# Stage one of an attention and mixture-of-experts layer: the input is also read in turned layout, and normalized there

## The chip, the core and the metric

The kernel runs on one core of one Trainium2 chip. TensorE (PE in the profile) multiplies matrices, VectorE (DVE) and ScalarE (ACT) work element by element, GpSimd (POOL) issues indirect DMAs and does some element work, and SyncE (SP) issues most DMAs. The metric is the device time of one execution in microseconds; lower is better.

## The reference, cut to what matters

```python
x = L0_attn_x                                    # (4, 2048, 512) f32
xn = _layernorm(x, axis=-1)                      # (x - mean) / sqrt(var + eps), over the 512 features
x = x + attention(xn, Wq, Wk, Wv, Wo) + moe(xn, gate_w, w_gate_up, w_down, ws_gate_up, ws_down)

# attention: q = xn @ Wq (16 heads of 32), k, v = xn @ Wk, xn @ Wv (4 heads), causal softmax, @ Wo
# moe:       logits = xn @ gate_w.T  -> best 3 of 8 groups -> softmax -> top 6 of 32 experts, 96 places each
#            + shared expert: silu(xn @ gs) * (xn @ us) @ ws_down
```

## The kernel before, in words

The 8192 tokens go through four stages: stage one (`stage_a`, to about 1100 us), the experts (`stage_m`, in part woven into what follows), attention (`stage_b`) and the output projection (`stage_c`). The change touches stage one alone.

Stage one goes over 16 chunks of 512 tokens. Chunk 0 and the last two are written out or run with their own flags; the others are one hardware loop. Every engine has its own program, and only semaphores order them. For a chunk TensorE multiplies the turned, normalized input (features on partitions, tokens along the row) with weights that stay in SBUF. All products are done in three terms of rounded f32: each operand is split into a high part (ACT copies it with rounding) and a low part (DVE subtracts the high part from the value), and the terms are high x high, high x low, low x high. In the order of TensorE's program, a chunk is:

- the gate logits (8 matmuls, `gate`), then V, four blocks of Q, and K (12 matmuls each, `product`), with two small groups of transposes (`smp`) in between;
- 11 products for the gate and up halves of the shared expert;
- the shared expert's down product: four groups of 17 matmuls into `yp`, one group for each 128 tokens, alternating between two PSUM banks. A group waits (`ysb_done`) until DVE has added the group two before it into `y_sb`.

The turned input of the next chunk is made during this last part. DVE has computed mean and variance of the next chunk's rows (`ln_stats`, `ln_variance`), the inverse deviation `rstd` (`ln_inverse`) and the normalized rows `xn` (`ln_scale`, line 577), 128 tokens on partitions by 512 features. `xn` is also written to DRAM for the experts. TensorE turns `xn` with 16 transposes of 128 x 128 (`transposes`, line 765) into the two PSUM banks `xtp`: eight ahead of the down product, eight between its second and third group. ACT rounds each 128 x 512 block of `xtp` into `x_hi` (line 449) once the chunk's last product has read the old `x_hi`; DVE subtracts it into `x_lo` (line 583). The next chunk's first matmul waits for all four blocks of `x_lo`.

SP's order in a chunk: load the rows of x to which the result is added (`y_sb`); store `qk_hi`, `qk_lo` (Q and K, five blocks of 128 x 512 each) and V; wait for `ln_done`; store `xn`; load the rows of the chunk after next; wait for DVE's additions; store the sum. POOL writes the expert table with 24 indirect DMAs a chunk.

Of the kernel before, what the change touches and what calls it, by code (L numbers as in the profile page):

```python
# [19 lines left out]
ALU = mybir.AluOpType  # L20
# [131 lines left out]
def stage_a(nc, t, car):  # L152

    ctx = ExitStack()
    with ctx:
# [107 lines left out]
        glu_done = sem("glu_done")  # L263
        hhi_done = sem("hhi_done")
        hlo_done = sem("hlo_done")
        xhi_done = sem("xhi_done")
        xlo_done = sem("xlo_done")
        ysb_done = sem("ysb_done")
# [35 lines left out]
        def earlier(n):  # L304

            return [m for m in range(n) if place[m] == place[n]]

        iota_e = cst[:, 0:E]
        tri = cst[:, E:E + NG * NG].rearrange("p (a b) -> p a b", b=NG)
        tok0 = cst[:, E + NG * NG:]  # L310
# [18 lines left out]
        def _(sp):  # L329
# [13 lines left out]
            def body(c, nxt, nxt2):  # L343
                sp.wait_ge(ysb_done, c * NT + 2)
                sp.sem_inc(sp_pass, 1)
                sp.dma_start(y_sb[:], chunk(x_d, c)).then_inc(xr_in, 16)
                if not nxt:
                    sp.wait_ge(xn_out, 16 * NC)
                    sp.wait_ge(xt_done, NC * KC)
                    load_weights(sp, t, 0, car["wgu0"], car["wdn0"], car["w_in"][0])  # L350
                sp.wait_ge(qlo_done, c * (NKV + 1) + NKV + 1)
                sp.sem_inc(sp_pass, 1)
                sp.wait_ge(qhi_done, c * (NKV + 1) + NKV + 1)
                sp.sem_inc(sp_pass, 1)
                sp.dma_start(columns(t["q_hi"], c), qk_hi[:, 0:NKV, :].bitcast(F32)).then_inc(qkv_out, 16)
                sp.dma_start(columns(t["q_lo"], c), qk_lo[:, 0:NKV, :].bitcast(F32)).then_inc(qkv_out, 16)
                sp.dma_start(columns(t["k_hi"], c), qk_hi[:, NKV:NKV + 1, :].bitcast(F32)).then_inc(qkv_out, 16)
                sp.dma_start(columns(t["k_lo"], c), qk_lo[:, NKV:NKV + 1, :].bitcast(F32)).then_inc(qkv_out, 16)
                sp.wait_ge(vt_done, c + 1)
                sp.sem_inc(sp_pass, 1)  # L360
                sp.dma_start(chunk(v_d, c), v_t[:]).then_inc(qkv_out, 16)
                if nxt:
                    sp.wait_ge(ln_done, c * NT + 2 * NT)
                    sp.sem_inc(sp_pass, 1)
                    sp.dma_start(chunk(xn_d, c + 1), xn[:]).then_inc(xn_out, 16)
                if nxt2:
                    sp.dma_start(x_sb[:], chunk(x_d, c + 2)).then_inc(x_in, 16)
                if not nxt:
                    sp.wait_ge(acc_done, NC * NACC)
                    for part in range(JC // 2):  # L370
                        load_qk(sp, t, car, 0, 0, part)
                if nxt:
                    sp.wait_ge(ysb_done, c * NT + NT + 2)
# [47 lines left out]
        def _(act):  # L421
# [20 lines left out]
            nc.scalar.activation(gw[:, :, 0:E], g_f[:], ACT.Copy).then_inc(g_hi_done, 1)  # L442
            whi(range(KC))

            def xhi(c, ks=range(KC)):

                for k in ks:
                    act.wait_ge(xt_done, c * KC + k + 1)
                    nc.scalar.activation(x_hi[:, k, :], xtp[:, k % 2, :], ACT.Copy).then_inc(xhi_done, 1)

            def logits(c):

# [43 lines left out]
                    xhi(c + 1)  # L496

            act.wait_ge(init_v, 1)
            xhi(0, (0, 1))
            whi(range(KC, NEAR))  # L500
            xhi(0, (2, 3))
            whi(range(NEAR, NEAR + 2))
            logits(0)
            whi(range(NEAR + 2, LATE))
# [11 lines left out]
        def _(dve):  # L516
# [54 lines left out]
            def ln_scale(c):  # L571
                dve.wait_ge(rstd_done, c * 5 + 5)
                dve.wait_ge(tab_init, 32)
                dve.wait_ge(xn_out, c * 16)
                dve.wait_ge(xt_done, c * KC)
# [4 lines left out]
            def xlo(c, ks=range(KC)):  # L580
                for k in ks:
                    dve.wait_ge(xhi_done, c * KC + k + 1)
                    V.tensor_tensor(x_lo[:, k, :], xtp[:, k % 2, :], x_hi[:, k, :].bitcast(F32),
                                    ALU.subtract).then_inc(xlo_done, 1)


# [13 lines left out]
            xlo(0, (0, 1))  # L600
            wlo(range(KC))
            xlo(0, (2, 3))
            wlo(range(KC, LATE))

            def body(c, nxt, begin=False):
# [127 lines left out]
                    for kst in car["kst"]:  # L733
                        V.memset(kst[R3:R3 + 1, :].bitcast(F32), 1.0).then_inc(init_v, 1)
                if nxt:
                    xlo(c + 1, (0, 1))
                dve.wait_ge(xr_in, c * 16 + 16)
                for i in range(NT):
                    if nxt and i == 2:
                        xlo(c + 1, (2, 3))  # L740
                    dve.wait_ge(y_done, c * NT + i + 1)
                    V.tensor_tensor(y_sb[:, i, :], yp[:, i % 2, :], y_sb[:, i, :], ALU.add).then_inc(ysb_done, 1)
# [9 lines left out]
        def _(pe):  # L752
            M = nc.tensor.matmul

            def transposes(c, ks=range(KC), begin=False):

                if not begin:
                    pe.wait_ge(ln_done, c * NT + NT)
                for k in ks:
                    if not isinstance(c, int) or c * KC + k >= 2:  # L760
                        pe.wait_ge(xlo_done, c * KC + k - 1)
                    for i in range(NT):
                        if begin and k == 0:
# [39 lines left out]
            def body(c, nxt):  # L803
# [23 lines left out]
                for n in range(2 * FM - 1):  # L827
# [11 lines left out]
                    released(c, FIRST_F + n)  # L839
                    pe.wait_ge(w_lo_done, split_by(C_GU + n * P))  # L840
                    product(c, FIRST_F + n, C_GU + n * P, P)
                if nxt:
                    transposes(c + 1, (0, 1))
                pe.wait_ge(w_lo_done, NPC)
                pe.wait_ge(hlo_done, c * FM + FM - 1)
                for i in range(NT):
                    if nxt and i == 2:
                        transposes(c + 1, (2, 3))
                    pe.wait_ge(ysb_done, c * NT + i + 1)
                    n = 0  # L850
                    for m in range(FM):
# [9 lines left out]
                    last.then_inc(y_done, 1)  # L861

            pe.wait_ge(cst_in, 48)
            transposes(0, begin=True)
            pe.wait_ge(init_v, 7)
            with pe.Fori(0, NC - 1) as c:
                body(c, True)
# [1036 lines left out]
def host_layout(np, a):  # L1904
# [3 lines left out]
    for m in range(FM):  # L1908
# [5 lines left out]
    return {"x": np.ascontiguousarray(a["L0_attn_x"]).reshape(T, D), "w_a": np.ascontiguousarray(w_a),  # L1914
            "w_d": np.ascontiguousarray(w_d), "w_g": w_g, "w_o": np.ascontiguousarray(a["L0_attn_Wo"]),
            "e_gu": np.ascontiguousarray(a["L0_ffn_w_gate_up"]), "e_d": np.ascontiguousarray(a["L0_ffn_w_down"])}

# [1 line left out]
def scratch(nc, out, dbg=()):  # L1919

    def dram(name, shape, dt):
# [5 lines left out]
            "tab": dram("tab_s", [E * CAP, 2], U32), "att": dram("att_s", [B, NKV, P, S], F32)}  # L1927


# [22 lines left out]
```

## Time and profile before

| | us |
|---|---|
| median of 3 runs | 3487.22 (3486.16 to 3487.94) |
| the profiled execution | 3486.41 |
| its span in the trace | 3484.7 |
| stage one, of it | to about 1100 |

The span is what the trace covers; 1.7 us of the profiled execution lie around it. In timelines a row gives the start of an instruction, its duration, and in brackets how long its engine sat idle before it and what released it. A TensorE matmul is recorded with its whole way through the array, so neighbouring matmuls overlap in the records (0.39 us each, one starting every 0.23 us): the pace is read from the starts.

### The profile page before, as it was taken

The page shows a single profiled execution, that of the slowest core. Times are in us where ns is not written, and L with a number is a line of the kernel's source. Part 1 is how long each engine was busy: PE and PEld are TensorE (multiplying, and loading weights), DVE is VectorE, ACT ScalarE, POOL GpSimd, SP SyncE. Part 2 cuts the span into 40 slices and gives each one's busy share as a digit, 9 for nine tenths or more (in the row PEclk, how much of TensorE's full clock was granted, in tenths as well). Part 3 has the DMA queues.
Part 4 walks back from the last instruction along what each step waited for, and adds up shares of the span by engine and source line. Part 5 has one row for each costly group of instructions (what it writes and reads, how often), then busy time and mean ns, then how long its engine had stood idle before and what let it go on. Part 6 is the DMA issues. An engine that isn't in the chain of part 4 may idle for free. (4 is left out here: it accounts for less than half of the span.)

```text
span 3484.7 us, 57392 instructions
## 1 busy us (share of the span) xinstructions
PE 3449.9 (99%) x19872; PEld 2226.5 (64%) x19872; DVE 2166.8 (62%) x5314; ACT 1603.9 (46%) x3331; POOL 2063.7 (59%) x1596
## 2 busy tenths in 40 slices
PE   8999999999999999999999999999999999999999
PEld 6888888888886555555555555555555555555487
DVE  6555455454544333777777777777777777777353
ACT  3232232222221112666666666666666666666611
POOL 1333332442334222878978897897889789878800
PEclk9999999999999999999999999999999999999999
DMA  5333233233325998232123203221220222030186
GB/s 184 106 115 106 94 104 119 90 106 115 106 97 180 324 305 241 44 71 63 32 60 69 62 24 72 64 52 36 68 62 27 68 69 62 23 81 26 42 305 245
DMA packets 259930, 358.68 MB, mean 103 GB/s; under 512 B 89676, under 2 KB 99404, under 8 KB 259720
## 3 DMA queue, kind: packets, MB, share of 16 engines
q1 hardware_dynamic: 232184, 325.72, 31.1%
q0 software_dynamic: 17920, 12.82, 1.8%
q10 hardware_dynamic: 9616, 17.46, 1.3%
q8 instruction: 117, 1.92, 0.2%
q14 instruction: 93, 0.76, 0.1%
HBM read 234.16 MB, written 121.38 MB: 102 GB/s over the span
## 5 line engine op out<-in xcount | busy, mean ns | idle before, releaser
L1559 ACT ACTIVATE prb<-banks 128x512 f32<-128x512 f32 (+3 forms) x2560 | 1158.6, 561 | 637.5 <-PE banks L1656 629.5
L1583 DVE TENSOR_REDUCE mx<-banks 128x1 f32<-128x512 f32 x1496 | 957.5, 681 | 333.6 <-PE banks L1641 333.5
L395 POOL DMA_INDIRECT tab_s<-pay,slot x384 | 376.6, 981 | 715.1 <-DVE tokf L708 479.1
L1501 POOL TENSOR_TENSOR rows<-rows,prb 128x1024 f32<-128x1024 f32 x252 | 597.0, 2395 | 0.0
L1586 DVE CUSTOM_DVE_ANT_0 banks<-banks,bias 128x384 f32<-128x384 f32 x981 | 498.4, 525 | 116.2 <-PE banks L1641 114.4
L1668 PE MATMUL ops<-prb,vst 128*32 128x512 f32 (+3 forms) x5120 | 557.2, 534 | 0.0
L1656 PE MATMUL banks<-w_hi,x_hi 97*128 97x512 f32 (+2 forms) x1280 | 494.3, 396 | 3.3 <-DVE ones_b L1576 1.7
L1656 PE MATMUL banks<-w_lo,x_lo 97*128 97x512 f32 (+2 forms) x1280 | 484.2, 395 | 1.3 <-ACT prb L1559 0.5
L1641 PE MATMUL banks<-x_lo,w_lo 96*128 96x512 f32 (+2 forms) x1280 | 463.5, 375 | 0.0
L1641 PE MATMUL banks<-x_hi,w_hi 96*128 96x512 f32 (+2 forms) x1197 | 436.8, 377 | 0.0
L774 PE MATMUL acc<-x_hi,w_hi 128*128 128x512 f32 x1088 | 429.0, 394 | 1.6 <-DVE qk_lo L610 1.6
L774 PE MATMUL acc<-x_lo,w_hi 128*128 128x512 f32 x1088 | 424.2, 390 | 0.0
L774 PE MATMUL acc<-x_hi,w_lo 128*128 128x512 f32 x1088 | 423.8, 390 | 0.0
L1656 PEld LDWEIGHTS banks<-w_hi,x_hi 97*128 97x128 f32 x1280 | 242.3, 189 | 212.8 <-issue 123.3
L1656 PEld LDWEIGHTS banks<-w_lo,x_lo 97*128 97x128 f32 x1280 | 239.4, 188 | 212.2 <-issue 114.6
L1495 POOL TENSOR_TENSOR rows<-prb 128x1024 f32<-128x1024 f32 x128 | 304.0, 2397 | 101.0 <-ACT prb L1559 101.0
L1482 POOL TENSOR_SCALAR_AFFINE_SELECT prb<-prb 128x256 f32<-128x256 f32 x512 | 200.4, 412 | 204.5 <-ACT prb L1559 201.3
L1501 POOL TENSOR_TENSOR third_sum<-third_sum,prb 128x1024 f32<-128x1024 f32 x124 | 296.4, 2391 | 0.0
L1668 PEld LDWEIGHTS ops<-prb,vst 128*32 128x32 f32 x5120 | 133.6, 109 | 250.0 <-ACT prb L1559 127.9
L1641 PEld LDWEIGHTS banks<-x_lo,w_lo 96*128 96x128 f32 x1280 | 242.6, 190 | 42.0 <-DVE mx L1583 20.2
L1641 PEld LDWEIGHTS banks<-x_hi,w_hi 96*128 96x128 f32 x1197 | 227.9, 191 | 40.7 <-DVE mx L1583 19.8
L774 PEld LDWEIGHTS acc<-x_hi,w_hi 128*128 128x128 f32 x1088 | 204.6, 188 | 46.1 <-DVE qk_lo L610 2.9
(174 smaller groups left out, 4206.6 us busy)
## 6 DMA issues: line engine op xcount, KB each, us to landing
wgu<-in_e_gu SPq DMA_DIRECT2D x24, 1408.0 KB, 7.1
xn_s<-rows SPq DMA_DIRECT2D x16, 1024.0 KB, 5.1
y_sb<-in_x SPq DMA_DIRECT2D x16, 1024.0 KB
q_hi_s<-qk_hi SPq DMA_DIRECT2D x16, 1024.0 KB, 4.2
q_lo_s<-qk_lo SPq DMA_DIRECT2D x16, 1024.0 KB, 6.5
base<-y_sb SPq DMA_DIRECT2D x16, 1024.0 KB, 4.3
w_hi<-q_hi_s SPq DMA_DIRECT2D x64, 256.0 KB, 6.0
w_lo<-q_hi_s SPq DMA_DIRECT2D x64, 256.0 KB, 6.3
```

Of the source, the lines that this page charges most:

```text
L395: nc.gpsimd.indirect_dma_start(t["tab"], bass.IndirectOffsetOnAxis(ap=slot[:, i, k:k + 1], axis=0), pay[:, i, k, :], None, bounds_check=E ...
L774: last = M(acc[0:width, i % ACCB, :], w[:, k, col:col + width], x[:, k, :], start=(n == 0), stop=(n == 3 * KC - 1))
L1482: nc.gpsimd.affine_select(out=blk, in_=blk, compare_op=ALU.is_ge, fill=0.0, base=0, pattern=[[0, 2], [1, P]], channel_multiplier=-1).then_ ...
L1495: nc.gpsimd.tensor_tensor(acc4, prb[:, slot(bg, f, pr)], prb[:, slot(bg, f + 1, pr)], ALU.add).then_inc(add_done, 1)
L1501: nc.gpsimd.tensor_tensor(acc4, acc4, prb[:, slot(bg, n, pr)], ALU.add).then_inc(add_done, 1)
L1559: nc.scalar.activation(prb[:, slot(bg, k, h // 2), h % 2, q0:CH], bank("score", bg, GROUP * k + h)[:, q0:CH], ACT.Exp, scale=SCALE).then_i ...
L1583: V.tensor_reduce(mx[:, h * NKT + qt, j:j + 1], held[:, 0:wr], AX.X, ALU.max).then_inc(mred_done, 1)
L1586: V.tensor_tensor_reduce(held[:, 0:wr], held[:, 0:wr], bias[:, CH - wr:CH], 1.0, LOWEST, ALU.add, ALU.max, mx[:, h * NKT + qt, j:j + 1]).t ...
L1641: M(bank("piece", bg, n)[:, 0:w], qst[p][0:R3, qt // NT, h, qt % NT * P:(qt % NT + 1) * P], kst[p][0:R3, k0:k0 + w], start=True, stop=True ...
L1656: M(bank("score", bg, u)[:, q0:CH], kst[p][0:R3 + 1, kt * P:(kt + 1) * P], qst[p][0:R3 + 1, j, h, q0:CH], start=True, stop=True).then_inc( ...
L1668: last = M(ops[HD * h:HD * (h + 1), q0:CH], vst[p][:, kt, :], prb[:, slot(bg, k, h // 2), h % 2, q0:CH], start=(kt == 0), stop=(r == 3), s ...
```

## The change

The host hands x over a second time, as `x_t`: for each chunk 128 partitions (feature within a block) by 4 blocks by 512 tokens. From chunk 1 on, the turned input is loaded instead of being made on TensorE:

- SP waits until the chunk's five stores of Q, K and V have landed, and loads the next chunk's `x_t` (1 MB) into the place of `qk_hi` (`xnt`). It waits for `rstd`, writes mean and `rstd` of the 512 tokens to a small DRAM array `ln` (two DMAs of 512 separate 4-byte numbers), waits until they have landed, and reads each of the two rows back on all 128 partitions (`mean_b`, `rstd_b`, in the place of `qk_lo`, 256 KB each). Only then come the wait for `ln_done`, the store of `xn` and the load of the rows of the chunk after next.
- DVE subtracts the mean and multiplies by `rstd` on `xnt`, block by block (`normalize`, eight 128 x 512 operations a chunk). Blocks 0 and 1 go ahead of the first addition into `y_sb`, their `x_lo` behind it; blocks 2 and 3 with their `x_lo` between the second and the third.
- ACT reads `x_hi` from `xnt` in SBUF, not from `xtp` in PSUM.
- TensorE's transposes stay for chunk 0 alone.

```diff
+        xnt = qk_hi[:, 0:KC, :].bitcast(F32)
+        mean_b, rstd_b = (qk_lo[:, n, :].bitcast(F32) for n in range(2))
...
@@ SP, body(c, nxt, nxt2)
                 sp.dma_start(chunk(v_d, c), v_t[:]).then_inc(qkv_out, 16)
                 if nxt:
+                    sp.wait_ge(qkv_out, c * 80 + 80)
+                    sp.sem_inc(sp_pass, 1)
+                    sp.dma_start(xnt, t["x_t"][c + 1] if isinstance(c, int) else
+                                 t["x_t"][ds(c + 1, 1)].rearrange("o p k s -> (o p) k s")).then_inc(xt_in, 16)
+                    sp.wait_ge(rstd_done, c * 5 + 10)
+                    sp.sem_inc(sp_pass, 1)
+                    with nc.allow_non_contiguous_dma(reason="a token's two numbers change places"):
+                        for n, column in enumerate((mv[:, :, 0], rstd[:])):
+                            sp.dma_start(t["ln"][n:n + 1].rearrange("o (i p) -> (o p) i", p=P),
+                                         column).then_inc(ln_out, 16)
+                    sp.wait_ge(ln_out, c * 32 + 32)
+                    sp.sem_inc(sp_pass, 1)
+                    sp.dma_start(mean_b, t["ln"][0:1].to_broadcast([P, CH])).then_inc(ln_in, 16)
+                    sp.dma_start(rstd_b, t["ln"][1:2].to_broadcast([P, CH])).then_inc(ln_in, 16)
                     sp.wait_ge(ln_done, c * NT + 2 * NT)
                     sp.sem_inc(sp_pass, 1)
                     sp.dma_start(chunk(xn_d, c + 1), xn[:]).then_inc(xn_out, 16)
...
@@ ACT
+            def xhi(c):
+
+                for k in range(KC):
+                    act.wait_ge(normed, c * KC + k + 1 - KC)
+                    nc.scalar.activation(x_hi[:, k, :], xnt[:, k, :], ACT.Copy).then_inc(xhi_done, 1)
...
@@ DVE
+            def normalize(c, ks):
+                for k in ks:
+                    V.tensor_tensor(xnt[:, k, :], xnt[:, k, :], mean_b, ALU.subtract).then_inc(centred, 1)
+                for k in ks:
+                    dve.wait_ge(centred, c * KC + k + 1 - KC)
+                    V.tensor_tensor(xnt[:, k, :], xnt[:, k, :], rstd_b, ALU.mult).then_inc(normed, 1)
+
+            def xlo(c, ks):
                 for k in ks:
                     dve.wait_ge(xhi_done, c * KC + k + 1)
-                    V.tensor_tensor(x_lo[:, k, :], xtp[:, k % 2, :], x_hi[:, k, :].bitcast(F32),
+                    V.tensor_tensor(x_lo[:, k, :], xnt[:, k, :], x_hi[:, k, :].bitcast(F32),
                                     ALU.subtract).then_inc(xlo_done, 1)
...
@@ DVE, body
                 if nxt:
-                    xlo(c + 1, (0, 1))
+                    dve.wait_ge(xt_in, c * 16 + 16)
+                    dve.sem_inc(dve_pass, 1)
+                    dve.wait_ge(ln_in, c * 32 + 32)
+                    dve.sem_inc(dve_pass, 1)
+                    normalize(c + 1, (0, 1))
                 dve.wait_ge(xr_in, c * 16 + 16)
                 for i in range(NT):
+                    if nxt and i == 1:
+                        xlo(c + 1, (0, 1))
                     if nxt and i == 2:
+                        normalize(c + 1, (2, 3))
                         xlo(c + 1, (2, 3))
                     dve.wait_ge(y_done, c * NT + i + 1)
                     V.tensor_tensor(y_sb[:, i, :], yp[:, i % 2, :], y_sb[:, i, :], ALU.add).then_inc(ysb_done, 1)
...
@@ PE, body
-                if nxt:
-                    transposes(c + 1, (0, 1))
                 pe.wait_ge(w_lo_done, NPC)
                 pe.wait_ge(hlo_done, c * FM + FM - 1)
                 for i in range(NT):
-                    if nxt and i == 2:
-                        transposes(c + 1, (2, 3))
                     pe.wait_ge(ysb_done, c * NT + i + 1)
...
@@ host_layout
+    x_t = np.ascontiguousarray(a["L0_attn_x"].reshape(NC, CH, KC, P).transpose(0, 3, 2, 1))
```

How the order of TensorE's program changes in the loop's chunk, at the start of the down product. Before (`xtp` is the turned input, `yp` the down product):

```order
L758 ISA
L761 REGISTER_ALU [waits ln_done]
L765 MATMUL xtp<-ident,rows 128x128 [waits xlo_done]
L765 MATMUL xtp<-ident,rows 128x128 x3
L765 MATMUL xtp<-ident,rows 128x128 [waits xlo_done]
L765 MATMUL xtp<-ident,rows 128x128 x3
L849 REGISTER_ALU [waits hlo_done,w_lo_done]
L858 MATMUL yp<-d_hi,h_hi 128x512 [waits ysb_done]
```

After:

```order
L821 MATMUL acc<-x_hi,w_lo 128x512
L892 REGISTER_ALU [waits hlo_done,w_lo_done]
L901 MATMUL yp<-d_hi,h_hi 128x512 [waits ysb_done]
L901 MATMUL yp<-d_hi,h_lo 128x512
L901 MATMUL yp<-d_lo,h_hi 128x512
```

Eight transposes and their waits are gone here, and eight more ahead of the third group; nothing else moves on TensorE in stage one.

DVE at the same place, from the end of the shared expert's last block. Before:

```order
L686 TENSOR_TENSOR h_hi<-four,h_hi 64x512 [waits hhi_done]
L582 REGISTER_ALU
L583 TENSOR_TENSOR x_lo<-xtp,x_hi 128x512 [waits xhi_done]
L582 REGISTER_ALU
L583 TENSOR_TENSOR x_lo<-xtp,x_hi 128x512 [waits xhi_done]
L737 ISA
L741 ISA [waits xr_in]
L742 TENSOR_TENSOR y_sb<-yp,y_sb 128x512 [waits y_done]
```

After (`qk_hi` holds `xnt`, `qk_lo` the two spread rows):

```order
L728 TENSOR_TENSOR h_hi<-four,h_hi 64x512 [waits hhi_done]
L778 ISA
L780 ISA [waits xt_in]
L617 TENSOR_TENSOR qk_hi<-qk_hi,qk_lo 128x512 [waits ln_in]
L617 TENSOR_TENSOR qk_hi<-qk_hi,qk_lo 128x512
L619 REGISTER_ALU
L620 TENSOR_TENSOR qk_hi<-qk_hi,qk_lo 128x512 [waits centred]
L619 REGISTER_ALU
L620 TENSOR_TENSOR qk_hi<-qk_hi,qk_lo 128x512 [waits centred]
L790 ISA [waits xr_in]
L791 TENSOR_TENSOR y_sb<-yp,y_sb 128x512 [waits y_done]
L624 REGISTER_ALU
```

Four operations and two DMA waits (`xt_in`, `ln_in`) now stand ahead of the first addition, on which TensorE's third group waits.

SP in the loop's chunk, after the change (before, L361's successor here was the wait for `ln_done`):

```order
L369 DMA v_s<-four 128x4x128
L371 ISA
L373 ISA [waits qkv_out]
L373 DMA qk_hi<-in_x_t 128x2048
L375 REGISTER_ALU
L379 DMA ln_s<-mv 128x4x1 [waits rstd_done]
L379 DMA ln_s<-rstd 128x4x1
L381 ISA
L383 DMA qk_lo<-ln_s 128x512 [waits ln_out]
L384 DMA qk_lo<-ln_s 128x512
L385 REGISTER_ALU
L387 DMA xn_s<-rows 128x4x512
```

The store of `xn` and the load behind it now come after three more waits of this queue.

## Rows read from the trace of the kernel before

**Rows 1.** The page: span; busy time by engine (share of span) xinstructions.

```profile
span 3484.7 us, 57392 instructions
...
PE 3449.9 (99%) x19872; PEld 2226.5 (64%) x19872; DVE 2166.8 (62%) x5314; ACT 1603.9 (46%) x3331; POOL 2063.7 (59%) x1596
```

**Rows 2.** Windows: PE, PEld, DVE, ACT, POOL busy (instructions), clock, DMA share, GB/s.

```profile
110.00:1000.00 890.00, 890.00 (x4203) 722.42 (x4202) 460.46 (x1110) 245.92 (x385) 306.67 (x314) 1.00 0.32 107
```

**Rows 3.** Tile xtp: duration ns min/median/max, first and last start, forms.

```profile
L765 PE MATMUL xtp<-ident,rows x256: 270/272/477, 12.7 to 1026.3; 128*128 128x128 f32 x128
L449 ACT ACTIVATE x_hi<-xtp x64: 572/592/598, 14.5 to 1026.7; 128x512 fp32r<-128x512 f32 x64
L583 DVE TENSOR_TENSOR x_lo<-xtp,x_hi x64: 680/691/693, 15.2 to 1027.4; 128x512 fp32r<-128x512 f32 x64
```

**Rows 4.** PE timeline, chunk 7's end: start us, us, engine line op, [idle <-releaser].

```profile
545.46 0.39 PE L774 MATMUL acc<-x_hi,w_lo 128*128 128x512 f32 x1
545.69 1.03 PE L765 MATMUL xtp<-ident,rows 128*128 128x128 f32 x8
546.48 0.48 PE L858 MATMUL yp<-d_hi,h_hi 128*128 128x512 f32 x1
546.80 0.41 PE L858 MATMUL yp<-d_hi,h_lo 128*128 128x512 f32 x1
```

**Rows 5.** PE timeline, middle of the same chunk's shared-down product.

```profile
554.51 1.04 PE L765 MATMUL xtp<-ident,rows 128*128 128x128 f32 x8
...
555.62 0.39 PE L858 MATMUL yp<-d_hi,h_lo 128*128 128x512 f32 x1
```

**Rows 6.** PE timeline, the last chunk, which turns nothing.

```profile
1083.93 0.40 PE L774 MATMUL acc<-x_hi,w_lo 128*128 128x512 f32 x1
1084.16 0.39 PE L858 MATMUL yp<-d_hi,h_hi 128*128 128x512 f32 x1
...
1093.12 0.49 PE L858 MATMUL yp<-d_hi,h_hi 128*128 128x512 f32 x1 [0.85 <-DVE y_sb L742]
```

**Rows 7.** DVE timeline, the same chunk 7 as rows 4.

```profile
534.78 0.16 DVE L569 TENSOR_TENSOR rstd<-rstd,nwt 128x4 f32<-128x4 f32 x1
...
548.15 0.69 DVE L686 TENSOR_TENSOR h_hi<-four,h_hi 64x512 fp32r<-64x512 f32 x1 [0.70 <-ACT h_hi L493]
548.87 1.29 DVE L583 TENSOR_TENSOR x_lo<-xtp,x_hi 128x512 fp32r<-128x512 f32 x2
550.75 0.69 DVE L742 TENSOR_TENSOR y_sb<-yp,y_sb 128x512 f32<-128x512 f32 x1 [0.59 <-PE yp L858]
554.71 0.69 DVE L742 TENSOR_TENSOR y_sb<-yp,y_sb 128x512 f32<-128x512 f32 x1 [3.27 <-PE yp L858]
...
563.51 0.69 DVE L742 TENSOR_TENSOR y_sb<-yp,y_sb 128x512 f32<-128x512 f32 x1 [3.27 <-PE yp L858]
568.51 0.43 DVE L615 TENSOR_REDUCE lg<-smp 128x128 f32<-128x256 f32 x1 [4.30 <-PE smp L818]
```

**Rows 8.** DVE timeline, the last chunk, beside rows 6.

```profile
1092.37 1.29 DVE L742 TENSOR_TENSOR y_sb<-yp,y_sb 128x512 f32<-128x512 f32 x2
```

**Rows 9.** SP timeline (DMA issues), chunk 7.

```profile
519.26 0.38 SPq L355 DMA_DIRECT2D q_hi_s<-qk_hi  x1
...
522.97 0.98 SPq L361 DMA_DIRECT2D v_s<-four  x1
...
537.79 0.39 SPq L367 DMA_DIRECT2D rows<-in_x  x1
```

**Rows 10.** DMA issues: out<-in engine op xcount, KB each, median us to landing.

```profile
y_sb<-rec_s SPq DMA_DIRECT2D x252, 64.0 KB, 2.0
rows<-in_x SPq DMA_DIRECT2D x15, 1024.0 KB, 7.4
...
tab_s<-pay,slot POOLq DMA_INDIRECT x384, 2.1
...
v_s<-four SPq DMA_DIRECT2D x16, 256.0 KB, 5.5
```

More of the change, by code:

```diff
@@ L265, in stage_a @@
         hlo_done = sem("hlo_done")
+        xt_in = sem("xt_in")
+        ln_out = sem("ln_out")
+        ln_in = sem("ln_in")
+        centred = sem("centred")
+        normed = sem("normed")
         xhi_done = sem("xhi_done")
@@ L348, in body @@
                     sp.wait_ge(xn_out, 16 * NC)
-                    sp.wait_ge(xt_done, NC * KC)
+                    sp.wait_ge(xt_done, KC)
                     load_weights(sp, t, 0, car["wgu0"], car["wdn0"], car["w_in"][0])
@@ L443, in _, with xhi_begin @@
             whi(range(KC))
-            def xhi(c, ks=range(KC)):
+            def xhi_begin(ks):
                 for k in ks:
-                    act.wait_ge(xt_done, c * KC + k + 1)
+                    act.wait_ge(xt_done, k + 1)
                     nc.scalar.activation(x_hi[:, k, :], xtp[:, k % 2, :], ACT.Copy).then_inc(xhi_done, 1)
+            def xhi(c):
+                for k in range(KC):
+                    act.wait_ge(normed, c * KC + k + 1 - KC)
+                    nc.scalar.activation(x_hi[:, k, :], xnt[:, k, :], ACT.Copy).then_inc(xhi_done, 1)
             def logits(c):
@@ L498, in _ @@
             act.wait_ge(init_v, 1)
-            xhi(0, (0, 1))
+            xhi_begin((0, 1))
             whi(range(KC, NEAR))
-            xhi(0, (2, 3))
+            xhi_begin((2, 3))
             whi(range(NEAR, NEAR + 2))
@@ L574, in ln_scale @@
                 dve.wait_ge(xn_out, c * 16)
-                dve.wait_ge(xt_done, c * KC)
+                if not isinstance(c, int) or c:
+                    dve.wait_ge(xt_done, KC)
                 for i in range(NT):
@@ L578, in ln_scale, with xlo_begin @@
                                     ALU.subtract, ALU.mult).then_inc(ln_done, 1)
-            def xlo(c, ks=range(KC)):
+            def xlo_begin(ks):
+                for k in ks:
+                    dve.wait_ge(xhi_done, k + 1)
+                    V.tensor_tensor(x_lo[:, k, :], xtp[:, k % 2, :], x_hi[:, k, :].bitcast(F32),
+                                    ALU.subtract).then_inc(xlo_done, 1)
+            def normalize(c, ks):
+                for k in ks:
+                    V.tensor_tensor(xnt[:, k, :], xnt[:, k, :], mean_b, ALU.subtract).then_inc(centred, 1)
+                for k in ks:
+                    dve.wait_ge(centred, c * KC + k + 1 - KC)
+                    V.tensor_tensor(xnt[:, k, :], xnt[:, k, :], rstd_b, ALU.mult).then_inc(normed, 1)
+            def xlo(c, ks):
                 for k in ks:
                     dve.wait_ge(xhi_done, c * KC + k + 1)
-                    V.tensor_tensor(x_lo[:, k, :], xtp[:, k % 2, :], x_hi[:, k, :].bitcast(F32),
+                    V.tensor_tensor(x_lo[:, k, :], xnt[:, k, :], x_hi[:, k, :].bitcast(F32),
                                     ALU.subtract).then_inc(xlo_done, 1)
@@ L599, in _ @@
             V.tensor_tensor(gw[:, :, E:2 * E], g_f[:], gw[:, :, 0:E].bitcast(F32), ALU.subtract).then_inc(g_lo_done, 1)
-            xlo(0, (0, 1))
+            xlo_begin((0, 1))
             wlo(range(KC))
-            xlo(0, (2, 3))
+            xlo_begin((2, 3))
             wlo(range(KC, LATE))
@@ L753, in _, with transposes @@
             M = nc.tensor.matmul
[L755 to L761, printed above, removed]
+            def transposes():
+                for k in range(KC):
+                    if k >= 2:
+                        pe.wait_ge(xlo_done, k - 1)
                     for i in range(NT):
-                        if begin and k == 0:
+                        if k == 0:
                             pe.wait_ge(ln_done, i + 1)
@@ L863, in _ @@
             pe.wait_ge(cst_in, 48)
-            transposes(0, begin=True)
+            transposes()
             pe.wait_ge(init_v, 7)
@@ L1913, in host_layout @@
     w_g = np.ascontiguousarray(a["L0_ffn_gate_w"].T.reshape(KC, P, E).transpose(1, 0, 2))
-    return {"x": np.ascontiguousarray(a["L0_attn_x"]).reshape(T, D), "w_a": np.ascontiguousarray(w_a),
+    x_t = np.ascontiguousarray(a["L0_attn_x"].reshape(NC, CH, KC, P).transpose(0, 3, 2, 1))
+    return {"x": np.ascontiguousarray(a["L0_attn_x"]).reshape(T, D), "x_t": x_t, "w_a": np.ascontiguousarray(w_a),
             "w_d": np.ascontiguousarray(w_d), "w_g": w_g, "w_o": np.ascontiguousarray(a["L0_attn_Wo"]),
@@ L1926, in scratch @@
             "den": dram("den_s", [2, GROUP, CH], F32), "rec": dram("rec_s", [2, GROUP, CH], F32),
-            "tab": dram("tab_s", [E * CAP, 2], U32), "att": dram("att_s", [B, NKV, P, S], F32)}
+            "tab": dram("tab_s", [E * CAP, 2], U32), "att": dram("att_s", [B, NKV, P, S], F32),
+            "ln": dram("ln_s", [2, CH], F32)}
 def kernel(**inputs):
```

## The prediction

> **What bounds the kernel now.** I read the page first: TensorE is busy for 99% of the span, every other engine for 64% or less [rows 1]. The windows say the same of stage one alone: from 110 to 1000 us TensorE is busy for the whole 890 us at a granted clock of 1.00 (2.4 GHz), DVE for 460, ACT for 246, and the DMA engines for 0.32 of it [rows 2]. So in stage one TensorE's own issue sets the time. What leaves its program shortens the chunk, and what is put on DVE, ACT or SP costs nothing until TensorE waits for it. The third thing to read is when each of the few hand-overs to TensorE comes, in the timelines of one chunk (chunk 7; the loop repeats it).
>
> **What leaves TensorE.** There are 256 transposes into `xtp` [rows 3], 16 for each of 16 chunks; 240 of them go. Their price is read from the starts. Eight begin at 545.69 and the second matmul of the down product starts at 546.80 [rows 4], 1.11 us for nine starts. The pace of the down product is (554.51 - 546.80)/33 = 0.2336 us a matmul [rows 4, 5]. Without the transposes the first matmul would stand at 545.69 and the second 0.2336 later, so the block costs 1.11 - 0.23 = 0.876 us: 0.79 for the transposes and 0.09 for a slower first matmul behind them. That this last bit goes too is seen in the last chunk, which turns nothing: the down product's first matmul starts at 1084.16, 0.23 after the product before it, and has the plain duration 0.39 instead of 0.48 [rows 6]. The second block, 554.51 to 555.62, is again 1.11 [rows 5], 0.876. A chunk gets 1.75 us back, 15 chunk boundaries 26.3 us.
>
> Here the duration column would mislead. It says 272 ns for a transpose [rows 3], 65 us for 240, but eight start within 0.79 us [rows 4], 99 ns apart. The Trainium skill (TensorE: Matmul & The Clock Gate, "Part 4: PE-mode transpose") gives about 275 ns for a 128x128 transpose in one kernel's context. By that page's figure, as an estimate, 240 of them would be 66 us; the trace agrees with it as a duration and not as a pace, and I go by the pace.
>
> **What DVE and ACT get.** DVE gets eight 128x512 operations a chunk. The nearest rows are L583 and L686, of the same size, 0.69 us alone and 1.29 for two in a row [rows 7]; 4 x 1.29 = 5.2 us a chunk. DVE's idle time between these rows, 0.59 + 3.27 + 3.27 + 4.30 = 11.4 us [rows 7], covers it. ACT only reads from another place, four times 0.59 as now [rows 3].
>
> What counts is the order. On this chunk's clock, with the transposes gone, the down product runs from 545.69; its third group is due after 34 matmuls, at 553.63, and the next chunk's first matmul after 68, at 561.57.
> - The third group needs the first addition into `y_sb`. In the last chunk, where TensorE does wait for it, the group starts 0.75 us after the addition starts (1092.37 to 1093.12) [rows 6, 8]. So the addition must start by 552.88. DVE is through with its block at 548.15 + 0.69 = 548.84 [rows 7]; then two subtractions 1.29, 0.1 for the hand-over (an estimate; the gap from 548.84 to 548.87 is 0.03), two multiplications 1.29: 551.5. That is 1.4 us ahead of the need.
> - ACT rounds blocks 0 and 1 by 552.2, DVE subtracts them by 553.5, adds the second group at about 553.9 and is free at 554.5. Blocks 2 and 3: 2.7 us to 557.2, ACT 0.59, the last `x_lo` at about 558.6. It is due at 561.57, 3.0 us later.
>
> So with the data there in time, TensorE waits nowhere.
>
> **Is the data there in time?** SP's new chain, on the same clock. V's store is issued at 522.97 and takes 0.98 to issue [rows 9] and 5.5 to land [rows 10]: the place of `qk_hi` is free at 529.5 at the latest. A 1 MB load takes 7.4 [rows 10]: `x_t` is in by 537.3, 11 us ahead of DVE. `rstd` is ready at 534.94 [rows 7]. The two stores of 512 single numbers have no row of their kind. To issue, the store of `qk_hi`, which also has 512 pieces, takes 0.38 [rows 9], so both are out by 535.8. To land, the nearest row is the table store, 128 pieces of 8 bytes in 2.1 [rows 10]. Low end: 2.1 for both together, 537.9. High end: all time is per piece, 4 x 2.1 = 8.4 each, one after the other, and only behind `x_t`: 537.3 + 16.8 = 554.1. I take 2.1 behind `x_t`, 539.4, since those pieces were spread by software over separate rows and still took 2.1. The two loads back: two issues 0.8, and 2.0 to land (64 KB from `rec_s`, a row spread over partitions in the same manner) up to 7.4 (1 MB) [rows 10]; for 256 KB I take 4. The numbers are there at 544.2, with ends at 540.7 and 562.3. DVE asks for them at 548.84, and TensorE feels them only past 548.84 + 1.4 = 550.2. Value taken: no cost, 6 us to spare. Far end: 12.1 us of wait a chunk.
>
> The Trainium skill (DMA: Bandwidth & Descriptors, "Rules for kernel authors") says that a non-contiguous last dimension becomes one descriptor for each element, and tells the author to rearrange. No row here shows what such a DMA costs. By that rule both stores are 512 descriptors each, which speaks against this change; the sum above bounds that case by the table store's row, so neither value of the sum moves.
>
> **What is moved on SP.** The store of `xn` and the load of the rows for the chunk after next, issued at 537.79 [rows 9], go behind the numbers' return, to about 545. The load lands 7.4 later, at 553. The statistics that read it stand on DVE behind the reduction at 568.51 [rows 7], 566.8 after the saving: 14 us of cover. The stored `xn` is asked for one chunk later. The added bytes (1 MB, 0.5 MB spread, a chunk) stand against a DMA share of 0.32 [rows 2]; none of TensorE's operands but the new ones come by DMA in stage one. The later stages have the same program and start earlier by what stage one saves.
>
> **The sum.** 3486.41 - 26.3 = 3460.1 for the profiled execution. The median of the runs is 0.8 above it, so 3487.22 - 26.3 = 3460.9; I say 3461.
>
> **Rivals.**
> 1. *The numbers come back late, and the kernel is slower.* The place is DVE's wait for `ln_in` ahead of the first addition, with TensorE's third group behind that. It decides from 550.2 + 1.75 = 552.0 on, that is when the way from `rstd` to DVE and back takes over 17 us. With 8.4 for the two stores together behind `x_t` and 7.4 for the loads it is 537.3 + 8.4 + 0.8 + 7.4 = 553.9: 3.7 late, less 1.75 saved, 15 times: +29, 3516. The far end is 12.1 - 1.75, 15 times: +155, 3642. For it: two dependent trips through DRAM with 4-byte pieces. Against it: the table store's 2.1 and the 2.0 of `rec_s` [rows 10].
> 2. *DVE is the late one.* The margin at the first addition is only 1.4 us. If the four operations ahead of it took 1.3 us each instead of 0.65, the addition would come 2.6 later and TensorE wait 1.2 a chunk: 18 us of the 26 lost, 3479; a little more and there is no gain, 3487. Against it: L686, all in SBUF, takes the same 0.69 as the rows that read PSUM [rows 7].
> 3. *A transpose is worth its full duration.* 240 x 0.272 = 65 us, 3421. The Trainium skill's figure above is the one that would say so. The eight starts within 0.79 us speak against it, and I keep it as a token.
>
> **How the numbers follow.** The forecast 0.86 (its own range 3457 to 3465: the runs of before spread over 1.8 us, and where stages two to four meet their waits may shift by as much); rival 1 0.06; rival 2 with part of the gain 0.05, with none of it 0.02; rival 3 0.01. Under 0.2% (7 us) a measurement of this kernel tells no difference. Faster: 0.86 + 0.05 + 0.01 = 0.92; same 0.02; slower 0.06. The range 3455 to 3468 is the forecast's with a few us on each side; what it leaves out is mainly rivals 1 and 2, 14 in 100.
>
> **What would show it.** Right: 16 records of transposes instead of 256; a chunk period of 65.5 us (now (1083.93 - 545.46)/8 = 67.3 from chunk 7 to 15 [rows 4, 6], less 1.75); the first matmul of the down product 0.23 behind the last product, with no idle time on TensorE for `y_sb` in the third group or for `x_lo` at the gate; DVE's normalization starting as soon as its block is through, not at a DMA. Wrong: idle time of DVE in front of the first subtraction that is released by a DMA, with TensorE waiting for `y_sb` each chunk (rival 1); the same wait of TensorE with no DMA ahead of it (rival 2); a pace of the products other than 0.23 us, which this working takes as given.

## The result, and the profile after

The changed kernel takes 3462.48 us (median of 4 runs, 3461.58 to 3463.23) against 3487.58 before (4 runs, 3486.16 to 3488.31). The ratio is 0.9931, 95% interval 0.9919 to 0.9942: 25.1 us less. The prediction said 3461, 3455 to 3468. The profiled execution's span is 3459.5 us, 25.2 less than [rows 1]. The 15 periods of stage one (a period is the distance between the first gate matmuls of two chunks) give 24.3 of it. 0.6 lies ahead of the first gate matmul, which starts at 19.48 here and at 20.09 before; the changed kernel run again (e8 below) has 19.98, so that isn't the change.

The page, then the windows of stage one (PE, PEld, DVE, ACT, POOL busy, clock, DMA share, GB/s), then the tile `xtp`:

```profile
PE 3423.6 (99%) x19632; PEld 2197.0 (64%) x19632; DVE 2237.5 (65%) x5434; ACT 1611.1 (47%) x3331; POOL 2081.8 (60%) x1596
```

```profile
110.00:1000.00 890.00, 889.59 (x4098) 716.23 (x4097) 534.96 (x1237) 256.77 (x395) 324.15 (x315) 1.00 0.40 133
```

```profile
L812 PE MATMUL xtp<-ident,rows x16: 421/421/477, 12.1 to 16.9; 128*128 128x128 f32 x16
```

TensorE is still busy all through stage one, with 240 matmuls fewer [rows 1, 3]; DVE got 75 us more work in 890 [rows 2] and the DMA share went from 0.32 to 0.40, and neither shows in the time as such.

TensorE's timeline at the end of chunk 7: the first gate matmuls of chunks 7 and 8 (their distance is the period), and between them the start of the down product:

```profile
483.84 0.40 PE L845 MATMUL acc<-x_hi,gw 128*64 128x512 f32 x1
...
533.27 0.39 PE L821 MATMUL acc<-x_hi,w_lo 128*128 128x512 f32 x1
533.50 0.45 PE L901 MATMUL yp<-d_hi,h_hi 128*128 128x512 f32 x1
533.79 0.40 PE L901 MATMUL yp<-d_hi,h_lo 128*128 128x512 f32 x1
...
549.42 0.40 PE L845 MATMUL acc<-x_hi,gw 128*64 128x512 f32 x1
```

The period is 65.58, and the down product starts 0.23 behind the last product, where eight transposes stood [rows 4]. The second matmul comes 0.29 later, not 0.23. The period was 67.29 in every chunk before. After, nine of the fourteen from chunk 1 to 15 are 65.57 or 65.58 and five are longer, up to 66.13; together the fourteen are 1.4 us over 14 x 65.57. Why is seen on DVE, same place as [rows 7]:

```profile
535.97 0.68 DVE L728 TENSOR_TENSOR h_hi<-four,h_hi 64x512 fp32r<-64x512 f32 x1 [0.70 <-ACT h_hi L521]
538.00 1.29 DVE L617 TENSOR_TENSOR qk_hi<-qk_hi,qk_lo 128x512 f32<-128x512 f32 x2 [1.35 <-DMA qk_lo<-ln_s]
539.21 1.29 DVE L620 TENSOR_TENSOR qk_hi<-qk_hi,qk_lo 128x512 f32<-128x512 f32 x2
540.53 0.69 DVE L791 TENSOR_TENSOR y_sb<-yp,y_sb 128x512 f32<-128x512 f32 x1
541.14 1.28 DVE L625 TENSOR_TENSOR x_lo<-qk_hi,x_hi 128x512 fp32r<-128x512 f32 x2
```

DVE waits 1.35 us for the spread numbers. Its first addition starts at 540.53; the prediction's limit, on this clock, is 533.50 + 34 x 0.2336 - 0.75 = 540.69. The margin that I put at 1.4 us, with 6 us more in front of it, is 0.16 us in this chunk. In chunk 9 it is gone:

```profile
669.83 1.29 DVE L617 TENSOR_TENSOR qk_hi<-qk_hi,qk_lo 128x512 f32<-128x512 f32 x2 [2.03 <-DMA qk_lo<-ln_s]
...
672.36 0.69 DVE L791 TENSOR_TENSOR y_sb<-yp,y_sb 128x512 f32<-128x512 f32 x1
```

```profile
673.11 0.50 PE L901 MATMUL yp<-d_hi,h_hi 128*128 128x512 f32 x1 [0.30 <-DVE y_sb L791]
```

The down product starts at 664.65 there, so the limit is 671.84; the addition is 0.52 late and the period 0.56 longer. So it goes all along: DVE waits for the numbers in each of the 15 chunks (0.14 to 2.03 us). In exactly the five chunks with a long period the addition starts past the limit, by 0.06 to 0.52 (the periods are 0.12 to 0.56 longer); in the nine others it starts 0.16 to 1.4 ahead of it.

SP's timeline of chunk 7 says where the margin went (issue of the two stores, then of the two loads that wait for their landing):

```profile
522.86 0.38 SPq L379 DMA_DIRECT2D ln_s<-mv  x1
523.29 0.50 SPq L379 DMA_DIRECT2D ln_s<-rstd  x1
533.46 0.33 SPq L383 DMA_DIRECT2D qk_lo<-ln_s  x1
533.84 0.43 SPq L384 DMA_DIRECT2D qk_lo<-ln_s  x1
```

From the end of the last store's issue to the first load's it is 9.67 us here, 7.7 to 10.2 over the 15 chunks, 8.8 on average. I call this the lag. The load of `x_t` isn't in the way: it is issued at 516.52, six us before the stores, and by the list of issues such a load lands in 4.9 us:

```profile
qk_hi<-in_x_t SPq DMA_DIRECT2D x15, 1024.0 KB, 4.9
```

The windows show that the DMA engines don't work in most of the lag:

```profile
523.00:525.60 2.60, 2.60 (x14) 2.13 (x13) 2.53 (x9) 0.42 (x1) 0.00 (x0) 1.00 0.19 2
525.60:533.00 7.40, 7.40 (x34) 6.15 (x33) 5.15 (x11) 1.86 (x3) 1.06 (x2) 1.00 0.00 0
```

The stores' packets are over by 525.6, then there are 7.4 us with nothing, and only then does the semaphore rise, at which SP goes on.

### The profile page after: what moved, and what is told of

It reads as the page before. It is cut to its first block and busy times, and to the rows that moved or that the text cites. A ratio compares the mean times of both kernels' runs of the same rounds, so it can differ in the third digit from the quotient of the medians.

```text
span 3459.5 us, 57219 instructions
## 1 busy us (share of the span) xinstructions
PE 3423.6 (99%) x19632; PEld 2197.0 (64%) x19632; DVE 2237.5 (65%) x5434; ACT 1611.1 (47%) x3331; POOL 2081.8 (60%) x1596
## 5 line engine op out<-in xcount | busy, mean ns | idle before, releaser
L417 POOL DMA_INDIRECT tab_s<-pay,slot x384 | 394.0, 1026 | 672.8 <-DVE tokf L750 478.0
```

Of the source, the lines that this page charges most:

```text
L417: nc.gpsimd.indirect_dma_start(t["tab"], bass.IndirectOffsetOnAxis(ap=slot[:, i, k:k + 1], axis=0), pay[:, i, k, :], None, bounds_check=E ...
```

## The experiments

They ran on several chips. The kernel before took 3505.8 us beside the first four, 3486.9 beside the next four and 3518.0 beside the last three; in the traces of the first and third group TensorE also stands some 12 to 17 us in the last chunk, in all but e9. No trace shows why, and there is none of the kernel before from those chips. So each ratio is to the kernel before on the same chip, and what happens in the loop is read from the periods, which agree across chips to 0.03 us where the work is the same.

**What the transposes are worth.** e1 takes them out of the kernel before and adds nothing; later chunks then work on what chunk 0 left in the banks.

```diff
+                        act.wait_ge(xlo_done, c * KC + k - 1)
...
-                if nxt:
-                    transposes(c + 1, (0, 1))
...
-                    if nxt and i == 2:
-                        transposes(c + 1, (2, 3))
```

The added wait keeps ACT off a bank that DVE still reads.

> The kernel before, with TensorE's transposes left out from chunk 1 on; ACT and DVE still read the turned banks, which keep what chunk 0 left there, so the input of later chunks isn't computed. Nothing is added. Theory (the whole change is the issue time of 240 transposes, 1.75 us a chunk, and what the change adds costs next to nothing): 3487.6 - 26.3 = 3461, and within 1.5 us of the changed kernel, with a chunk period of 65.5 to 65.6. Rival (the transposes were worth more and the added work gives some of it back): clearly below the changed kernel's 3462.5, 3455 or less.

Ratio 0.9923 (0.991 to 0.9937), periods of 65.59 to 65.61:

```profile
483.93 0.40 PE L801 MATMUL acc<-x_hi,gw 128*64 128x512 f32 x1
...
549.53 0.39 PE L801 MATMUL acc<-x_hi,gw 128*64 128x512 f32 x1
```

Taking the transposes out is worth 1.69 us a chunk, and the whole change reaches 65.57 (65.60 in e8) where nothing is late. The theory holds; the rival would have needed a shorter period than the changed kernel's.

e2 puts them back into the changed kernel, writing banks that nobody reads.

```diff
+                if nxt:
+                    turn_again(c + 1, (0, 1))
...
+                    if nxt and i == 2:
+                        turn_again(c + 1, (2, 3))
```

> The changed kernel, with the transposes put back in their old places, into the banks that nobody reads any more. Theory: each chunk gets its 1.75 us back, the period is 67.3 again, 3462.5 + 26 = 3488 to 3489, and as the third group then starts 0.88 us later, TensorE's few waits for y_sb in the loop are gone. Rival (part of the gain came from reading x in SBUF in place of PSUM, or from the moved work on DVE and ACT): it stays clearly under the kernel before, 3480 or less.

Ratio 1.0015 (1.0006 to 1.0025): the gain is gone. From chunk 1 on thirteen periods are 67.28 or 67.29 and one is 67.56; TensorE has no wait for `y_sb` in the loop. The interval lies just above 1; the loop doesn't show that, and the last chunk, where TensorE stands 12 us in this trace, may.

```profile
496.64 0.40 PE L853 MATMUL acc<-x_hi,gw 128*64 128x512 f32 x1
...
563.93 0.40 PE L853 MATMUL acc<-x_hi,gw 128*64 128x512 f32 x1
```

With both, the loop's gain is TensorE's issue time for the transposes and nothing else.

**Where the lag comes from.** e4 adds a third store of the same kind.

```diff
-                        for n, column in enumerate((mv[:, :, 0], rstd[:])):
+                        for n, column in enumerate((mv[:, :, 0], rstd[:], rstd[:])):
```

> The changed kernel, with a third store of 512 numbers (the inverse deviation once more, to a row that nobody reads) ahead of the wait for the stores. Theory (the lag goes with the number of 4-byte pieces, 4 to 5 us for 512, and TensorE's third group is at its limit already): DVE gets the numbers 4 to 5 us later, TensorE waits 4 to 5 us for y_sb in each of 15 chunks, 3462.5 + 60 to 75 = 3522 to 3538, slower than the kernel before. Rival (the lag is a fixed latency of the last landing): the third store costs its 0.5 us of issue, TensorE waits 0.4 a chunk, 3469.

Ratio 0.9953 (0.9938 to 0.9967), still faster than before: the theory that the lag goes with the number of pieces is wrong. The lag is 9.4 us on average after 1.5 times the pieces; periods are 65.56 to 67.34, on average 0.6 us longer than the changed kernel's. That is near the rival's 0.4: the third store's own issue of 0.5 and a lag 0.6 longer.

e5 leaves one store of the two, e6 keeps both and sends each number to a place of its own. The rows that DVE reads come in part (e5) or wholly (e6) from constants. e5:

```diff
-                        for n, column in enumerate((mv[:, :, 0], rstd[:])):
+                        for n, column in ((1, rstd[:]),):
...
-                    sp.dma_start(mean_b, t["ln"][0:1].to_broadcast([P, CH])).then_inc(ln_in, 16)
+                    sp.dma_start(mean_b, t["flat"][0:1].to_broadcast([P, CH])).then_inc(ln_in, 16)
```

e6:

```diff
-                            sp.dma_start(t["ln"][n:n + 1].rearrange("o (i p) -> (o p) i", p=P),
+                            sp.dma_start(t["ln"][n:n + 1, :, 0].rearrange("o (i p) -> (o p) i", p=P),
...
-            "ln": dram("ln_s", [2, CH], F32)}
+            "ln": dram("ln_s", [2, CH, P], F32)}
```

> The changed kernel, with the inverse deviations stored alone, by one DMA of 512 numbers; the mean isn't stored, a constant row of zeros is spread in its place, so later chunks are not centred. So far: two such stores land 8.4 to 10.7 us after the second is issued, three hardly later (9.6 us), one store of 32-byte pieces within 1.2. Theory 1 (each 4-byte store drags on by itself, side by side with the others, 512 small writes into one 2 KB row that have to follow one another): one store alone still takes 8 us or more. Theory 2 (the stores share one slow path with a total of 1024 pieces, and the third was short by chance): one store alone lands in 4 to 5 us.

> The changed kernel, with the same two stores of 512 numbers of 4 bytes, but each number goes to a place 512 bytes from the next; the spread rows come from a constant (zeros and ones), so later chunks are not normalized. Theory 1 (the lag comes from many small writes into the same few stretches of DRAM): the lag falls to 3 us or less. Theory 2 (the lag comes from the pieces as such, wherever they land): it stays at 8 to 10 us.

One execution each, 3459.6 and 3460.0 us. SP's rows of e5 and then of e6, chunk 7:

```profile
523.32 0.38 SPq L379 DMA_DIRECT2D ln_s<-rstd  x1
531.45 0.34 SPq L383 DMA_DIRECT2D qk_lo<-in_flat  x1
```

```profile
522.83 0.38 SPq L379 DMA_DIRECT2D ln_s<-mv  x1
523.26 0.50 SPq L379 DMA_DIRECT2D ln_s<-rstd  x1
525.24 0.35 SPq L383 DMA_DIRECT2D qk_lo<-in_flat  x1
```

One store alone still lags 7.75 to 10.3 us (8.5 on average). The same 1024 pieces, 512 bytes apart in DRAM, lag 1.5 to 1.9 (1.6 on average). So it is not the number of pieces as such: it is 512 4-byte writes into the same 2 KB, and the stores drag side by side. e6's numbers are also read back by nobody, but e3's and e7's below are, and those lag little too. What in the memory makes the writes slow, whether they follow one another for one, the runs don't show. That the lag alternates between about 8 and 10 from chunk to chunk in the changed kernel also stays open.

The Trainium skill (DMA: Bandwidth & Descriptors, "Specifications") says that below 512 bytes the DMA does a read-modify-write. e6 has pieces of 4 bytes too and hardly lags, so that rule alone doesn't give these times.

**Packing the numbers.** e3 stores mean and inverse deviation side by side, 128 pieces of 32 bytes, and reads them on DVE with a stride of 32 bytes.

```diff
+        pairs = qk_lo[:, 0:2, :].bitcast(F32).rearrange("p a s -> p (a s)")
+        mean_b, rstd_b = (pairs.rearrange("p (q i t) -> p t i q", i=NT, t=2)[:, n] for n in range(2))
...
+                    sp.dma_start(t["ln"].rearrange("o (p j) -> (o p) j", p=P),
+                                 mv[:].rearrange("p i t -> p (i t)")).then_inc(ln_out, 16)
```

> The changed kernel, with mean and inverse deviation side by side for each row, stored by one DMA of 128 pieces of 32 bytes and read back by one; DVE reads them from the spread row with a stride. Theory (the lag of 8 to 10 us of the two stores comes from their 1024 pieces of 4 bytes): the way from rstd to DVE falls from 15 to some 7 us, DVE no longer waits for a DMA, the period is 65.55 in every chunk, and about 1.4 us is won, 3461, hardly to be told apart from 3462.5. Rival 1 (the lag is a latency of dependent DRAM traffic, whatever the pieces): DVE still waits 1 to 2 us and the time stays. Rival 2 (the strided reads slow DVE): the eight operations take well over 0.69 us and TensorE waits for y_sb, 3475 or more.

Ratio 0.9956 (0.9939 to 0.9972). The lag is 1.15 us (1.9 once), and rival 2 came true beside the theory: DVE's operations take 1.17 us where the changed kernel's take 0.685, the addition starts 0.45 to 0.49 past the limit, and thirteen of the fourteen periods are 66.1, with TensorE waiting about 0.25 us for `y_sb` (the record of the matmul before covers the rest). The other is 73.9: ACT is idle for 7.9 us in the middle of the products and TensorE stands too; nothing in the edit explains it. That the packed kernel is worse than the change rests on the periods, 0.5 us each, for the intervals of the two ratios overlap.

```profile
L618 DVE TENSOR_TENSOR qk_hi<-qk_hi,qk_lo x60: 1151/1167/1183, 77.1 to 1018.3; 128x512 f32<-128x512 f32 x60
```

```profile
L617 DVE TENSOR_TENSOR qk_hi<-qk_hi,qk_lo x60: 675/685/753, 78.7 to 1003.0; 128x512 f32<-128x512 f32 x60
```

The Trainium skill (SBUF — State Buffer, "Door 1: The DMA port swizzle") says that SBUF has lines of 16 bytes, that each access that crosses to a new line pays, and that a stride of up to four f32 values is free. A stride of 32 bytes is past that; the trace agrees, with 1.7 times the duration.

e7 avoids both. From chunk 1 on partition p holds tokens 4p to 4p+3, so the numbers leave in pieces of 16 bytes and come back in token order; the two long memsets of the last chunk go behind its additions. e8 is the changed kernel again, on the same chip in the same rounds.

```diff
+        xp_d = t["x"].rearrange("(c p t) d -> c p t d", p=P, t=NT)
...
+                    sp.dma_start(t["ln"].rearrange("n (p i) -> p n i", p=P), pair[:]).then_inc(ln_out, 16)
...
+                V.tensor_copy(pair[:, 0, :], mv[:, :, 0])
...
-                    dve.wait_ge(acc_done, NC * NACC)
-                    for kst in car["kst"]:
-                        V.memset(kst[R3:R3 + 1, :].bitcast(F32), 1.0).then_inc(init_v, 1)
...
+                    if not nxt and i < 2:
+                        dve.wait_ge(acc_done, NC * NACC)
+                        V.memset(car["kst"][i][R3:R3 + 1, :].bitcast(F32), 1.0).then_inc(init_v, 1)
```

> The changed kernel, mended in three places: from chunk 1 on partition p of the rows holds tokens 4p to 4p+3 instead of every 128th, so that mean and inverse deviation, put side by side in one small tile, go out by one DMA in 256 pieces of 16 bytes and come back in token order, and DVE reads them without a stride; and in the last chunk the two long memsets stand behind the first and second addition. Theory (the two 4-byte stores cost a margin and 1.4 us in all, the stride of the packed kernel cost DVE 0.47 us an operation): DVE has its numbers 8 us before it asks, eight operations of 0.69 us, every period from chunk 1 on is 65.57, TensorE's wait of 0.85 us in the last chunk is gone, 2.2 us under the changed kernel in the trace of stage one, ratio to it about 0.9994, not to be told apart by the time. Rival (the other order of the rows costs something: DMA, POOL's gathers): periods above 65.6 or a longer stage two, as long as the changed kernel or longer.

> The changed kernel itself, on the same chip as the mended one and in the same rounds. Both theories: 0.993 of the kernel before, periods of 65.57 with a few of up to 66.1.

e7: 3458.05 us (3456.78 to 3460.59), ratio 0.9921 (0.9907 to 0.9934). e8: 3461.29 (3460.71 to 3466.16), ratio 0.9934 (0.992 to 0.9947). All five runs of e7 are under all five of e8, the medians 3.2 us apart, though the ratios' intervals overlap. The lag is 1.3 to 2.6 us, all fourteen periods are 65.59 to 65.63 (e8: thirteen of them 65.59 to 65.62, and one of 65.91), and the wait of 0.85 us in the last chunk [rows 6] is gone. From the first gate matmul to the start of stage two the traces differ by 1.7 us; the other 1.5 of the medians I can't place.

**The margin on DVE.** Two more subtractions ahead of the normalization, in the changed kernel (e10) and in e7 (e11).

```diff
+                if ks[0] == 0:
+                    for k in ks:
+                        V.tensor_tensor(qk_lo[:, 2 + k, :].bitcast(F32), qk_lo[:, 0, :].bitcast(F32),
+                                        qk_lo[:, 1, :].bitcast(F32), ALU.subtract)
```

> The changed kernel, with two more 128x512 subtractions on DVE (into a free part of qk_lo, for nobody) ahead of the normalization of blocks 0 and 1, 1.2 us more in front of the first addition. Theory (DVE's margin of 1.4 us was used up by its wait for the 4-byte stores): in the chunks in which the stores land late (lag over 9 us, about every second one) TensorE waits about 1.1 us more for y_sb, 6 to 12 us in all, 3468 to 3474. Rival (DVE has room; late numbers aren't what sets the margin): periods stay at 65.57 to 66.1, 3462.

> The mended kernel with the rows in token order, with the same two subtractions more on DVE at the same place. Theory: its numbers are there long before, the whole margin of 1.4 us is free, and 1.2 us more go in: periods stay at 65.6, TensorE waits nowhere in the loop, the same time as the mended kernel, 3458. Rival (the margin has nothing to do with the stores): the same loss as in the changed kernel with two more, 6 to 12 us.

e10: ratio 0.9967 (0.9948 to 0.9986). Periods are 66.1 to 66.5 or 67.3 to 68.4, nearly in turn, 20 us over 14 x 65.6, more than the 6 to 12 I expected: here the lag was 0.5 us longer on average, and the chunks with the short lag lose 0.5 to 0.9 us too. The limit holds here as well: in twelve of the fourteen the period is longer by just what the addition starts past it, within 0.05 us; in the other two a second, smaller wait of TensorE comes on top. e11: ratio 0.9904 (0.9874 to 0.9935), periods of 65.60 to 65.65, no wait of TensorE in the loop. DVE's rows at the same place, e10 and then e11:

```profile
551.08 1.29 DVE L618 TENSOR_TENSOR qk_lo<-qk_lo 128x512 f32<-128x512 f32 x2 [2.25 <-DMA qk_lo<-ln_s]
552.29 1.28 DVE L621 TENSOR_TENSOR qk_hi<-qk_hi,qk_lo 128x512 f32<-128x512 f32 x2
```

```profile
536.96 1.29 DVE L620 TENSOR_TENSOR qk_lo<-qk_lo 128x512 f32<-128x512 f32 x2
538.17 1.28 DVE L623 TENSOR_TENSOR qk_hi<-qk_hi,qk_lo 128x512 f32<-128x512 f32 x2
```

The same 1.2 us of work costs the changed kernel 19 us (its fourteen periods had 1.4 over already) and e7 0.2. The stores are what used the margin up.

**Past the limit.** e9 makes the way longer by one more pair of stores.

```diff
-                    sp.wait_ge(ln_out, c * 32 + 32)
+                    sp.wait_ge(ln_out, c * 64 + 32)
...
+                        for n, column in enumerate((mv[:, :, 0], rstd[:])):
+                            sp.dma_start(t["ln"][n:n + 1].rearrange("o (i p) -> (o p) i", p=P),
+                                         column).then_inc(ln_out, 16)
+                    sp.wait_ge(ln_out, c * 64 + 64)
```

> The changed kernel, in which SP stores the two rows of numbers, waits until they have landed, stores them once more, waits again and only then reads them back: the way from rstd to DVE is longer by one store of 8 to 10 us. Theory (TensorE's third group waits for everything past a limit that the changed kernel already stands at): DVE's numbers come 9.7 us later, TensorE waits 8.5 to 9.7 us for y_sb in each of 15 chunks, periods of 74 to 75.5, about 3462 + 135 = 3597, slower than the kernel before. Rival (part of a late arrival is absorbed, because x_lo is due only 8 us after the third group): under 5 us a chunk, 3535 or less.

Ratio 1.0461 (1.0427 to 1.0495): slower than before, as rival 1 has it. The period is 78.7 on average, 13.1 more, where 8.5 to 9.7 were expected. TensorE waits 10.8 us a chunk for `y_sb` (139.8 us in 13 of them), and it resumes more slowly:

```profile
488.37 0.79 PE L907 MATMUL yp<-d_hi,h_hi 128*128 128x512 f32 x1 [10.82 <-DVE y_sb L797]
488.96 0.63 PE L907 MATMUL yp<-d_hi,h_lo 128*128 128x512 f32 x1
489.39 0.63 PE L907 MATMUL yp<-d_lo,h_hi 128*128 128x512 f32 x1
```

```profile
470.00:477.00 7.00, 7.00 (x32) 5.63 (x31) 1.66 (x3) 0.82 (x2) 5.21 (x6) 1.00 0.09 1
477.00:488.30 11.30, 0.55 (x3) 0.11 (x1) 3.17 (x6) 1.23 (x2) 4.50 (x5) 0.62 0.61 191
488.40:492.00 3.60, 3.60 (x9) 2.83 (x10) 3.60 (x7) 0.05 (x1) 0.00 (x0) 0.50 0.31 116
```

After 10.8 us of standing still the granted clock is 0.50 (1.2 GHz) and a matmul starts every 0.43 us; from 493.23 on, 4.9 us after the wait ended, it is 0.23 again. Ten matmuls at 0.2 us more are 2 us, which with the wait makes the 13.

## Why the prediction was right, step by step

- *What bounds the kernel, and the price of a transpose.* Right. 0.876 us for a block of eight, read from the starts, gave 1.75 a chunk; e1 measures 1.69, the quiet chunks of the changed kernel 1.72. The difference between 1.75 and 1.69 is the down product's second matmul, which comes 0.29 and not 0.23 behind the first. In the last chunk, from which the working took its 0.23, it does come 0.23 behind; in the loop, with the transposes gone, it doesn't, so most of the "last bit" of 0.09 stayed in the first block. The changed kernel's other 0.03 is the difference of pace between its trace and e1's or e8's. The 272 ns of the duration column would have given 65 us; e1 and e2 rule rival 3 out.
- *DVE's eight operations at 0.69 and their order.* Right: pairs of 1.29, and 2.53 us from the first to the addition. The limit, 0.75 us from the addition to the third group, is right too: it gives each late chunk's loss, and e11 shows that without late numbers the margin holds 1.2 us more. ACT's copies take 0.63 from SBUF, 0.59 from PSUM.
- *`x_t` in time, the moved store and load covered.* Right; no wait shows. `x_t` lands before the two stores are issued, so the case "behind `x_t`" didn't arise.
- *Is the data there in time?* This is the term that was mis-sized. For the stores' landing I took 2.1 us, the table store's row [rows 10], behind `x_t`; measured are 8 to 10. The far end of 16.8 for both covered it. "No cost, 6 us to spare" was wrong: DVE waits for a DMA in every chunk, which is the working's own sign of rival 1, and only TensorE's part of that sign stayed away in most. In the chunk shown the conclusion held by 0.16 us: the numbers were there at 538.0, on the old clock 550.2, exactly the limit that the text gives, and not 544.2. That the delay stopped there was luck; e10, with a lag 0.5 us longer and 1.2 us more on DVE, lost most of the gain. The table store's pieces go to places spread over the table, these 512 into one 2 KB row. The two stores differ in more than that, but of what the stores do e6 changes just the spacing, and the lag goes. The rule on descriptors that I weighed pointed the right way, but e6 has as many 4-byte pieces and hardly lags.
- *The sum.* 26.3 forecast, 25.1 measured. The loop's 15 periods give only 24.3: of the 2.0 that lack, 1.4 are the late numbers, a share of rival 1 that I had priced as all or nothing, and 0.5 the price of the transposes (1.72 for 1.75). The total came closer because the traces also differ by 0.6 ahead of the first gate matmul, which is chance, and by 0.3 outside the loop that I can't place.
- *Rival 1* is real: e9 shows its place and that it ends slower. Its price left a term out, since the idle time also costs TensorE its clock: 2 us a chunk after 10.8 of waiting, and in chunk 0 of e10 the granted clock is 0.50 from 86.5 to 89 after a wait of 2.6. *Rival 2* did not happen in the changed kernel, whose operations take 0.685; e3, at 1.17, shows it, and e10 that its margin had gone.

## What to carry to other kernels

When one engine is busy all through a stage, price what leaves it by the distance between starts and not by the durations, and check with a kernel that only leaves it out. A change that is right on time can still stand at its limit: compute the limit of each new hand-over and look in the profile after for how far it is kept, since 1.2 us more work on another engine cost 19 us here. For a small row that goes through DRAM, don't write numbers that land near each other one by one (pieces of 16 and 32 bytes were enough here), and choose the layout of the rows so that neither the store nor the later read needs a stride.

## What the runs showed of the hardware that was not expected

- A DMA of 512 pieces of 4 bytes into one 2 KB row of DRAM raises its semaphore 7.7 to 10.3 us after issue, though the DMA engines are done after 2.3; one, two or three such DMAs at once take about the same (8.5, 8.8, 9.4). With the pieces 512 bytes apart it is 1.6, with 128 pieces of 32 bytes in order 1.15, with 256 of 16 bytes 1.3 to 2.6. The last two have fewer pieces as well as larger ones, and the runs don't separate these.
- A 128x512 f32 operation of DVE, all in SBUF, takes 0.685 us, and 1.17 with one operand at a stride of 32 bytes.
